# Sandwich block (linear attention and experts) on one core: projected rows normalised out of PSUM, both halves in one slot, and a new order of the first block

## The reference

```python
def _layernorm(x, eps=1e-05):                       # no weights
    return (x - mean(x)) / sqrt(var(x) + eps)

# attention: B, S, HID, H, D = 2, 4096, 256, 8, 32, chunks of 64 rows
q, k, v = x @ Wq.T, x @ Wk.T, x @ Wv.T              # each reshaped to (b, s, H, D)
o = chunked_linear_attn(q, k, v)                    # causal, a running state k.T v per head
denom = maximum(abs(sum(q * cumsum(k))), 1.0)
o = rmsnorm(o / denom, norm_w)                      # over D
out = o.reshape(b, s, 256) @ Wo.T
# experts: 8 of them, inner width 256, all computed for every row
h = silu(x @ Wg[e]) * (x @ Wu[e]);  out = sum_e weights[e] * (h @ Wd[e])

x = x + _layernorm(attention(_layernorm(x)))
x = x + _layernorm(experts(_layernorm(x)))
```

## Time and profile before

| | |
|---|---|
| time of the profiled execution | 1508.8 us |
| its span, first to last instruction | 1507.1 us |
| mean granted TensorE clock | 0.994 |
| PE busy | 1468.6 us, 97% |
| DVE busy | 997.0 us, 66% |
| ACT busy | 680.4 us, 45% |
| POOL busy | 453.7 us, 30% |

### The profile page before, as it was taken

How to read it: one execution, slowest core, us unless ns; L and a number is a source line. 1 busy time by engine, 2 the same in 40 slices (tenths; PEclk the granted TensorE clock), 3 DMA queues, 4 the chain that set the end, 5 groups by cost and what they waited for, 6 DMA issues and landing times. The chain is left out here.

```text
span 1507.1 us, 37448 instructions
## 1 busy us (share of the span) xinstructions
PE 1468.6 (97%) x14436; PEld 1280.9 (85%) x14436; DVE 997.0 (66%) x2388; ACT 680.4 (45%) x1261; POOL 453.7 (30%) x720
## 2 busy tenths in 40 slices
PE   7799999999999999999999999999999999999997
PEld 6678888888888888888888888888888888888886
DVE  4646766666676766766666676766766666776765
ACT  4543544445344453545445344453535445344433
POOL 1422512234141332512234141332513234141231
PEclk9999999999999999999999999999999999999999
DMA  3300000000000000000000000000000000000000
GB/s 113 112 1 2 21 7 14 14 14 14 0 14 14 14 14 0 21 7 14 14 14 14 0 14 14 14 14 0 25 3 14 14 14 14 0 14 16 2 8 22
DMA packets 25345, 24.59 MB, mean 16 GB/s; under 512 B 2016, under 2 KB 25056, under 8 KB 25312
## 3 DMA queue, kind: packets, MB, share of 16 engines
q1 hardware_dynamic: 25312, 24.13, 5.0%
HBM read 15.74 MB, written 8.39 MB: 16 GB/s over the span
## 5 line engine op out<-in xcount | busy, mean ns | idle before, releaser
L677 ACT ACTIVATE h_hi<-late 128x512 fp32r<-128x512 f32 x256 | 161.6, 631 | 271.7 <-DVE late L956 271.5
L956 DVE TENSOR_TENSOR late<-late,up_ps 128x512 f32<-128x512 f32 x256 | 175.4, 685 | 158.0 <-PE up_ps L422 100.6
L422 PE MATMUL down_ps<-w_hi,h_hi 128*128 128x256 f32 x976 | 264.5, 293 | 0.0
L422 PE MATMUL down_ps<-w_hi,h_lo 128*128 128x256 f32 x976 | 253.9, 282 | 0.0
L758 ACT ACTIVATE late<-gate_ps 128x512 f32<-128x512 f32 x256 | 151.9, 593 | 220.9 <-PE gate_ps L422 216.3
L1164 POOL TENSOR_TENSOR rms_in<-rms_in,minus_half 128x16 f32<-128x16 f32 x32 | 93.8, 2930 | 510.7 <-DVE rms_in L920 510.7
L978 DVE SCALAR_TENSOR_TENSOR late<-down_ps,route,late 128x256 f32<-128x256 f32 x364 | 158.6, 477 | 105.6 <-PE down_ps L422 102.7
L871 DVE TENSOR_TENSOR h_lo<-late,h_hi 128x512 fp32r<-128x512 f32 x256 | 175.5, 685 | 64.7 <-ACT h_hi L677 64.7
L422 PE MATMUL gate_ps<-ft_hi,w_hi 128*128 128x512 f32 x512 | 204.3, 399 | 0.7 <-ACT ft_hi L677 0.4
L422 PE MATMUL gate_ps<-ft_hi,w_lo 128*128 128x512 f32 x512 | 203.0, 397 | 0.0
L422 PE MATMUL up_ps<-ft_hi,w_hi 128*128 128x512 f32 x512 | 199.3, 389 | 0.0
(11 more groups left out here) (161 smaller groups left out, 2571.6 us busy)
## 6 DMA issues: line engine op xcount, KB each, us to landing
xs<-in_x SPq DMA_DIRECT2D x32, 256.0 KB, 2.9
out_rows<-late SPq DMA_DIRECT2D x32, 256.0 KB, 2.2
late<-in_wg SPq DMA_DIRECT2D x8, 256.0 KB, 3.3
late<-in_wu SPq DMA_DIRECT2D x8, 256.0 KB, 2.7
late<-in_wd SPq DMA_DIRECT2D x8, 256.0 KB, 3.0
late<-in_wkv_t SPq DMA_DIRECT2D x1, 512.0 KB, 5.4
late<-in_wq_t SPq DMA_DIRECT2D x1, 256.0 KB, 4.6
late<-in_wo_t SPq DMA_DIRECT2D x1, 256.0 KB, 4.7
```

Of the source, the lines that this page charges most:

```text
L422: last = nc.tensor.matmul(dst, lhs, rhs, start=n == 0, stop=n == len(terms + low_terms) - 1)
L677: return nc.scalar.activation(dst, src, ACT.Copy)
L956: nc.vector.tensor_tensor(h_f[:, m, :], h_f[:, m, :], up_ps[m][:, :], ALU.mult).then_inc(h_ready[0], 1)
```

## The change

1. **Layer norm 2.** The output weights are scaled with the norm weights as before and then centred once, each row of Wo.T less its own mean over the outputs, so that every projected row has mean zero. The copy of the projected rows by ScalarE, `ln2_apply` and the shift go. VectorE takes the moments from PSUM, GpSimd computes only the root (`root_only`), and `ln2_add` is one scalar_tensor_tensor per tile out of PSUM: rows x rstd + x.
2. **Slots.** `ot 0` and `ot 1` stand together in slot 18, `wo 0` and `wo 1` in slot 20, both `ln2_stats` with `ln2_add 0` and `ln3_stats 0` in slot 21, `ln2_add 1` in 22, `ln3_stats 1` in 23.
3. **The first block** has an order of its own for each engine. x is loaded and transposed by halves of rows, `xt`, `q` and `kv` work on a half, VectorE normalises (`normalise`), and units also pass through two places of `x1`, eight in all.
4. **The last block.** GpSimd adds half 0; VectorE centres and adds half 1.

```diff
@@ STEPS
     [("norm_apply", 0)],
-    [("ot", 0)],
+    [],
     [("norm_apply", 1), ("carry",)],
-    [("wo", 0), ("ot", 1)],
-    [("ln2_stats", 0)],
-    [("wo", 1), ("ln2_apply", 0)],
-    [("ln2_stats", 1), ("ln2_add", 0), ("ln3_stats", 0)],
+    [("ot", 0), ("ot", 1)],
     [],
-    [("ln2_apply", 1), ("ln2_add", 1), ("ln3_stats", 1)],
+    [("wo", 0), ("wo", 1)],
+    [("ln2_stats", 0), ("ln2_stats", 1), ("ln2_add", 0), ("ln3_stats", 0)],
+    [("ln2_add", 1)],
+    [("ln3_stats", 1)],
     [("ln3_apply", 0)],
     [("ln3_apply", 1)],
@@ one list per engine for the first block
+FIRST_PE = [("xt", 0), ("kv", 0), ("q", 0), ("xt", 1), ("su", 0), ("kv", 1), ("kt", 0), ("kt", 1), ("s", 0), ("q", 1), ...
+FIRST_WARM = {("kv", 0): 6, ("s", 1): 2, ("o", 1): 5, ("ot", 0): 5, ("wo", 0): 6, ("ot", 1): 3, ("wo", 1): 6, ("ft", 0): 20}
@@
-            READ_OUT["wo", p] = (wo_copied, p + 1)
+            READ_OUT["wo", p] = (x1_ready, p + 1)
@@ staging places; 6 and 7 lie in x1
+        STAGES = [4, 5, 6, 7, 1, 2, 0, 3] * 2 + [4, 5, 0, 1, 2, 3, 4, 5]
@@ SyncE
+            load_first(0)
+            sp.dma_start(wkv_raw, ...).then_inc(att_w_loaded[1], 16)
+            load_first(1)
+            sp.dma_start(wq_raw, ...).then_inc(att_w_loaded[0], 16)
@@ ScalarE
-                elif kind == "wo":
-                    p = step[1]
-                    copy(rows[:, 2 * p:2 * p + 2, :], src)\
-                        .then_inc(wo_copied[0], 1)
...
-            act.wait_ge(w_ready, ATT_W + UNITS - 2)
+            act.wait_ge(w_ready, ATT_W + 20)
@@ VectorE
                 elif kind == "ln2_stats":
                     p = step[1]
-                    reach(dve, wo_copied, a, p + 1)
-                    ln_stats(2, rows, range(2 * p, 2 * p + 2), bn2, mv2)
+                    reach(dve, att_done, a, number_of(("wo", p), a) + 1)
+                    for b in range(B):
+                        last = nc.vector.bn_stats(bn2[:, 2 * p + b, :], att_half(("wo", p), a)[:, b, :])
+                    settle(last)
+                    for t in range(2 * p, 2 * p + 2):
+                        last = nc.vector.bn_aggr(mv2[:, t, :], bn2[:, t, :])
+                    last.then_inc(moments_ready[1][0], 1)
                 elif kind == "ln2_add":
-                    reach(dve, ln2_applied, a, p + 1)
+                    reach(dve, rstd_ready[1], a, p + 1)
                     reach(dve, x1_copied, a, 0)
-                    nc.vector.tensor_tensor(x1[:, ts, :], rows[:, ts, :], xs[:, ts, :], ALU.add).then_inc(x1_ready[0], 1)
+                    for b in range(B):
+                        t = 2 * p + b
+                        last = nc.vector.scalar_tensor_tensor(x1[:, t, :], att_half(("wo", p), a)[:, b, :], rstd2[:, t:t + 1],
+                                                              xs[:, t, :], ALU.mult, ALU.add)
+                    last.then_inc(x1_ready[0], 1)
...
+                    for g in range(HG):   # after the scaling by norm_w, and bn_stats and bn_aggr of the rows
+                        last = nc.vector.tensor_scalar(wo_raw[:, g, :], wo_raw[:, g, :], mv4[:, g, 0:1], None, ALU.subtract)
+                    last.then_inc(wo_scaled, 1)
@@ VectorE, last block, after both out_stats
-            for p in range(2):
-                out_add(nc.vector, dve, p, f)
+            for t in range(2, 4):
+                last = nc.vector.tensor_scalar(fin[:, t, :], fin[:, t, :], mv4[:, t, 0:1], None, ALU.subtract)
...
+                last = nc.vector.scalar_tensor_tensor(x1_kept[:, t, :], fin[:, t, :], rstd4[:, t:t + 1], x1_kept[:, t, :],
+                                                      ALU.mult, ALU.add)
@@ GpSimd
+            def root_only(n, p, a, mv, var, rstd):
+                ts = slice(2 * p, 2 * p + 2)
+                reach(pool, moments_ready[n - 1], a, p + 1)
+                settle(nc.gpsimd.tensor_tensor(var[:, ts], mv[:, ts, 1], ln_eps[:, ts], ALU.add))
+                nc.gpsimd.tensor_tensor(rstd[:, ts], var[:, ts], minus_half[:, 0, ts], ALU.pow).then_inc(rstd_ready[n - 1][0], 1)
```

More of the change, by code:

```diff
@@ new lines @@
+FIRST_DVE = [("x_stats", 0), ("x_norm", 0), ("low", "wkv"), ("xt", 0), ("x_stats", 1), ("scale", "wo"), ("low", "wq"),
+             ("x_norm", 1), ("low", "wo"), ("xt", 1), ("unit", 0), ("su", 0), ("unit", 1), ("unit", 2), ("unit", 3), ("unit", 4),
+             ("unit", 5), ("unit", 6), ("s", 0), ("unit", 7), ("unit", 8), ("su", 1), ("unit", 9), ("norm_stats", 0), ("s", 1),
+             ("unit", 10), ("unit", 11), ("unit", 12), ("unit", 13), ("norm_apply", 0), ("norm_stats", 1), ("unit", 14),
+             ("ot", 0), ("unit", 15), ("unit", 16), ("unit", 17), ("norm_apply", 1), ("ln2_stats", 0), ("ot", 1), ("ln2_add", 0),
+             ("ln3_stats", 0), ("ln2_stats", 1), ("unit", 18), ("ln2_add", 1), ("ln3_stats", 1), ("ln3_norm", 0), ("unit", 19),
+             ("ln3_norm", 1), ("ft_out", 0), ("ft_out", 1), ("unit", 20), ("unit", 21), ("unit", 22), ("unit", 23)]
@@ L346, in unit_src, with unit_raw, unit_loads, stage_free @@
             return (wg, wu, wd)[u % 3][u // 3, :, :].rearrange("(k p) n -> p k n", p=P)
-        def stage(u):
-            n = (u + 4) % NSTAGE
-            return n, late[:, 512 * n:512 * n + 512].rearrange("p (k n) -> p k n", k=2)
+        STAGES = [4, 5, 6, 7, 1, 2, 0, 3] * 2 + [4, 5, 0, 1, 2, 3, 4, 5]
+        def unit_raw(u):
+            n = STAGES[u]
+            flat = late[:, 512 * n:512 * n + 512] if n < 6 else x1[:, 2 * n - 12:2 * n - 10, :].rearrange("p t n -> p (t n)")
+            return flat.rearrange("p (k n) -> p k n", k=2)
+        def unit_loads(u):
+            return 16 * STAGES[:u + 1].count(STAGES[u])
+        def stage_free(u):
+            earlier = [v for v in range(u) if STAGES[v] == STAGES[u]]
+            return ATT_W + earlier[-1] + 1 if earlier else {1: 1, 2: 1, 0: 2, 3: 3}.get(STAGES[u], 0)
         wq_raw = late[:, 0:512].rearrange("p (k n) -> p k n", k=KT)
@@ L695, in att_step @@
                 kind = step[0]
-                if step in PSUM_STEPS and kind not in ("s", "su", "ft"):
+                if step in PSUM_STEPS and kind not in ("s", "su", "wo", "ft"):
                     reach(act, att_done, a, number_of(step, a) + 1)
                     src = att_half(step, a)
+                half = slice(2 * P * step[1], 2 * P * step[1] + 2 * P) if len(step) > 1 else None
                 if kind == "xt":
-                    copy(halves(xt_hi[:, step[1], :]), src).then_inc(xt_hi_ready[0], 1)
+                    copy(xt_hi[:, :, half] if is_first(a) else halves(xt_hi[:, step[1], :]), src).then_inc(xt_hi_ready[0], 1)
                 elif kind == "q":
-                    copy(q_t[:, step[1], :], src).then_inc(q_ready[0], 1)
+                    copy(q_t[:, :, half] if is_first(a) else q_t[:, step[1], :], src).then_inc(q_ready[0], 1)
                 elif kind == "kv":
@@ L733, in att_step @@
                         .then_inc(ft_hi_ready[0], 1)
-                elif kind == "ln2_apply":
-                    p = step[1]
-                    ln_apply(2, p + 1, a, rows, rows, range(2 * p, 2 * p + 2), shift2, rstd2).then_inc(ln2_applied[0], 1)
                 elif kind == "ln3_apply":
@@ L889, in att_step @@
                     k = step[1]
+                    half = slice(2 * P * k, 2 * P * k + 2 * P)
+                    lo, hi = (xt[:, :, half] if is_first(a) else halves(xt[:, k, :]) for xt in (xt_lo, xt_hi))
                     reach(dve, xt_hi_ready, a, k + 1)
-                    low(halves(xt_lo[:, k, :]), att_half(step, a), halves(xt_hi[:, k, :])).then_inc(xt_ready[0], 1)
+                    low(lo, att_half(step, a), hi).then_inc(xt_ready[0], 1)
                 elif kind == "s":
```

309 lines of the change are left out of this document (171 added, 138 removed).

## The result

The changed kernel took 1527.38 us (median of four runs, 1524.90 to 1529.81), the kernel before 1507.48 (1507.42 to 1509.41). The ratio is 1.0129, 95% interval 1.0106 to 1.0151: 1.3% slower. The forecast was 1519, the range 1504 to 1532. The profiled execution took 1529.35 us, with a span of 1527.6.

A forecast was written before the change was run, and what follows sets the result against it. The prediction took TensorE to bound the middle, so only its waits cost time. From the profiled 1508.8 us: middle +25.5, first block -13.5, tail -0.7 gives 1520.1, less 1.3 to the median's scale: 1519 us, range 1504 to 1532.

The forecast's parts named there:

- The main mechanism: Middle blocks: pieces added to VectorE's list between `down(5, 0)` and `low_hidden(6, 1)` exceed 0.38 us of slack, so TensorE waits.
- Which wait comes, and its size: Middle block: TensorE starts `down(6, 0)` 2.0 to 2.4 us later than 425.14, taken as 2.2.
- The wait for the root: Middle block: VectorE, through at 421.94, waits for GpSimd's root before `ln2_add 0` and goes on at 422.25 to 422.6.
- The wait at ft: Middle block: TensorE arrives 2.2 us later, so its wait at `ft` goes, giving back 0.37 to 0.59, taken as 0.5.
- The net per block: Middle block: 1.7 us slower after the `ft` gain, over 15 blocks +25.5 us (21 to 30.5).
- Reading in PSUM costs nothing: Middle block: VectorE reading projected rows from PSUM costs nothing; the skill's table would add 0.26 us per block, 3.9 in all.
- The first block: Start of the program: `up(0, 0)` starts at 55.0 instead of 69.55 us, a gain of 13.5 us (9 to 16).
- the forecast of the low clock: First block: `kv 0` runs its 12 products at the low clock, taking 5 us, to 15.
- twenty handovers: First block: some twenty handovers between engines take 1 us off the 14.5 us gain.
- the second rival: Middle blocks: the clock falls at each new wait, 22 us more, 1541 us, or in part of the blocks; chance 0.12.
- its partial case: Middle blocks: the clock falls behind the new wait in only a part of the blocks, 1530 us.
- The tail: After the last product: GpSimd's add of 1.30 us ends at 1503.0 and issues 0.4 later, -0.7 us (0 to -1.2).

The follow-up runs named there:

- two more statistics: Kernel before plus two unused pieces of statistics on VectorE between `ln2_add 0` and `ln3_stats 0` in each middle block: 1549.8 us, ratio 1.0275.
- slots apart: Changed kernel with the middle block's slots spread nearly as before the change, all else kept: 1503.9 us, ratio 0.9973 to the kernel before.
- ot 1 first: Changed kernel with the middle block's slots spread nearly as before, and `ot 1` ahead of `wo 0` in slot 18: 1490.3 us, ratio 0.9885.
- first block: On top of "ot 1 first": first block reordered on ScalarE and VectorE, identity passes at the start and before `up(0, 0)` changed: 1489.0 us, ratio 0.9876.
- Tail on VectorE: On top of "first block": the last block's first half is added on VectorE instead of GpSimd: 1488.8 us, ratio 0.9872.
- the two delays of VectorE: Kernel before plus two or three unused pieces of statistics on VectorE per middle block: 1549.8 us (ratio 1.0275) and 1574.6 us (1.0442).

## Why the prediction was nearly right, point by point

The main mechanism, VectorE's list that makes TensorE wait at `down(6, 0)`, is right, with its size. That 1527.4 also lies inside the forecast's own 1511 to 1529 is luck: that sum has no term for the clock, and the clock cost 7.8 us more in the profiled execution. Without it the time would have been close to the 1519 only because two errors nearly cancel: the first block came out 3 us longer than forecast, and the middle 2.1 us shorter.

- **Which wait comes, and its size: right.** Forecast: `down(6, 0)` 2.0 to 2.4 us later than 425.14. From VectorE's start on the add_down of `down(5, 0)` to `down(6, 0)` it was 6.73 us and is 426.03 - 417.29 = 8.74: 2.01 later, and 0.11 for the slow first product. VectorE's list was put at 8.7 to 9.1 us and is 8.61.
- **The wait for the root: smaller than said.** 0.2 us instead of 0.3 to 0.66: GpSimd began 0.1 us behind the moments and its first instruction took 0.20, not the 0.56 of the earlier trace rows.
- **The wait at ft: right in the changed kernel** (gone, 0.55 given back, 0.5 forecast). But the reason in the prediction, that TensorE arrives later, is only half of it: in "two more statistics" TensorE is late too, and the wait stays. It takes the add in front as well: with the add behind, 0.43 us of it came back.
- **The net per block**: 1.7 forecast, 1.56 measured; 23.4 us instead of 25.5.
- **Reading in PSUM costs nothing: right.** A pair of bn_stats takes 0.73 to 0.76 us out of PSUM (above) and 0.75 out of SBUF. The figures of the Trainium skill ("VectorE: DVE Perf Modes", the section on the TRN2 errata), by which (an estimate, 2 x 0.065) the pair would take 0.13 us more, don't hold here. What the prediction didn't see is that the *longer holding* of the PSUM half has a price. The changed kernel doesn't pay it, since with both `ot` steps ahead of both `wo` steps `wo 1` takes the half of `ot 1`; "slots apart" pays 0.81 us per block. The grouping that costs the 2.1 us thus avoids another wait; "ot 1 first" avoids both.
- **The first block: 3 us short.** -13.5 forecast, -10.45 measured, inside the bounds. "`kv 0` starts at 9.8" was wrong: it was 11.52, because TensorE stood at the 14 passes on the identity until 9.41, which I had left out of its queue. This cost nothing in the end, since the forecast of the low clock was wrong as well: at a granted 1.00 `kv 0` took 3.05 us instead of 5 and ended at 14.57 instead of 15. What delayed `kv 1` (19.88, 18.7 forecast) is the centring ahead of `wq_lo`, put down as hidden behind `kv 0`: `q 0` waited 1.45 us for it, to 16.02, and in "first block", where `wq_lo` stands ahead of the centring, `kv 1` came 1.47 us earlier. The largest loss came later. The second root, due at 38.1, began at 40.93, and `ot 1` came at 45.50 (about 42 forecast), `ft 1` at 57.69 (53.7). My 1 us for twenty handovers was too low for these 4 us; how much of them is handovers and how much is work that I left out isn't shown.
- **The clock: the step that failed.** I had given the second rival, that the clock falls at each new wait or at some, 0.12, and put its partial case at 1530. It is what happened: four falls in 15 blocks, 6.3 us. Behind `up(0, 0)` the clock cost 1.5 us more than before, which varies from one execution to the next. The argument against the rival, that 1.9 us of idle time is less than 2.43, was no reason: 1.85 us was enough, and with the wait filled the falls were gone. With these 7.8 us and the first block's 3 us, less 2.1 in the middle, the distance from the forecast span of 1518.4 (1507.1 + 11.3) to 1527.6 is 8.7 of 9.2.
- **The tail**: -0.7 forecast, -0.5 measured. The add pair on VectorE takes 1.80 us, not 0.87, beside GpSimd's add. "Tail on VectorE" shows that GpSimd is the cause. The Trainium skill ("SBUF — State Buffer", section "SBUF: two separate sides") states that VectorE with two inputs in SBUF and GpSimd share a pair of ports which the one that starts first holds for a whole instruction; the trace agrees: GpSimd's add starts first, 0.14 us ahead, and ends at 1523.95, and 0.87 us from there would be 1524.8, against a measured end of 1524.64.

## What to carry to other kernels

Before a piece is moved, add up what stands on the feeding engine between the last thing that it waits for and the first thing that the bounding engine waits for: an engine that is idle for a third of the time had 0.38 us of slack there. When a copy is dropped, ask who frees the buffer now, and give the next user another one. Price a wait of TensorE by starts, idle time plus 0.18 to 0.28 us here, and allow for a fall of the clock behind it (1.57 us in 4 of 15 blocks after 1.85 us). If the wait must stay, try cheap passes in it: both profiled executions with them kept the clock in the middle. And compare the middle blocks by their period, as the first block alone can move the time by 3 us.

## What the runs showed of the hardware that was not expected

- A wait of TensorE cost more than its idle time each time: 0.55 us for 0.37, 0.81 for 0.53, 2.11 for 1.85.
- Equal waits in equal blocks don't have equal results for the clock. Among 15 blocks it fell in none after waits of 0.53 and 1.07 us, in 4 after 1.85, in 4 after 2.05 and in 11 after 3.35, each time to the 1.2 GHz level for about 3 us of dense products. A fall cost 1.57 us in the changed kernel, and 0.87 and 0.85 us where a later wait took up the rest. These counts are of one profiled execution each, and for 0.53 and 1.07 us no other execution of the kernel had a higher mean clock than that one, so none isn't the same as never; the four executions of the changed kernel had a mean clock of 0.995 at spans of 1523.2 and 1523.7 us, and 0.991 to 0.992 at 1527.6 and 1528.1. The blocks with a fall are 1, 3, 9 and 14 in the changed kernel. With the two delays of VectorE they are regular: every fourth block (2, 6, 10, 14) after 2.05 us, and all but every fourth (3, 7, 11, 15) after 3.35 us. So which block falls isn't pure chance; what sets it is open.
- Two scalar_tensor_tensor of VectorE took 1.80 us instead of 0.87 beside one tensor_tensor of GpSimd.
